# Planning, first projections and linear attention of a graph layer: three stages or one

## What is computed

```python
xn = layernorm(x)
# tconv, twice, relu between: q, k, v, s = x @ Wq + bq, ...; e = edge_attr @ We
#   logits = (q[dst] * (k[src] + e)) per head / 8; softmax over the edges of dst
#   agg = sum over edges of (v[src] + e) * a;  result = agg + s
gnn = tconv(relu(tconv(xn, ...1)), ...2)
# linear attention, 4 heads of 32
k = softmax over all nodes of (xn @ Wk_mix);  context = k^T v, per head
mix = ((xn @ Wq_mix) * 32**-0.5 @ context) @ W_out + b_out
x = x + gnn + mix
x = x + moe(layernorm(x))          # 8 experts, 2 per node
```

## Time and profile before

| | us |
|---|---|
| median of 3 runs | 4657.78 |
| the profiled execution, whole | 4652.28 |
| its span in the trace | 4650.3 |
| plan, from its first DMA issue | 2.67 to 84.59 |
| first projections | to 340.51 |
| linear attention | to 474.91 |
| first edge stage | to 2119.34 |
| second projections | to 2362.22 |
| second edge stage and experts | to the end |

### The profile page before, as it was taken

The page is one execution under the profiler, slowest core; times in us unless marked ns, Lnnn a source line. Parts: engine busy times, 40 slices in busy tenths (PEclk is TensorE's granted clock), DMA queues, the critical chain, the costliest instruction groups (busy, mean ns, idle before and its releaser), DMA issues. The chain is left out here.

```text
span 4650.3 us, 105757 instructions
## 1 busy us (share of the span) xinstructions
PE 4196.0 (90%) x19410; PEld 3412.2 (73%) x19411; DVE 3781.8 (81%) x8580; ACT 2965.7 (64%) x10488; POOL 2773.8 (60%) x2804
## 2 busy tenths in 40 slices
PE   1987899999999999997889999999999999569994
PEld 0545788888888888873368888888888888359993
DVE  3444799999999999994569999999999999755443
ACT  0111478878888878883138887887888888535331
POOL 1000777777777777760058777777777777143465
PEclk9998999999999999998999999999999999769997
DMA  4434877777777777753477777777777777252344
GB/s 78 138 131 147 236 223 226 223 216 226 223 219 221 222 215 225 225 172 111 142 214 229 220 224 214 223 225 215 221 224 223 219 226 220 93 173 78 108 139 122
DMA packets 590944, 887.02 MB, mean 191 GB/s; under 512 B 111925, under 2 KB 455797, under 8 KB 590166
## 3 DMA queue, kind: packets, MB, share of 16 engines
q0 software_dynamic: 150656, 488.11, 35.7%
q1 hardware_dynamic: 397302, 340.56, 25.3%
q10 hardware_dynamic: 42336, 51.40, 3.0%
HBM read 788.70 MB, written 91.03 MB: 189 GB/s over the span
## 5 line engine op out<-in xcount | busy, mean ns | idle before, releaser
L871 POOL DMA_INDIRECT edge_kv<-kvD,edge_ix x1760 | 1745.1, 992 | 735.4 <-issue 455.2
L918 ACT ACTIVATE edge_w<-edge_vj,edge_ex 128x64 f32<-128x64 f32 x7040 | 1857.3, 335 | 364.8 <-PE edge_pa L959 357.3
L936 PE MATMUL edge_ps<-edge_We,edge_ea 112*128 112x256 f32 x7040 | 1837.5, 383 | 43.1 <-DMA edge_ea<-ea_t_dram 17.6
L936 PEld LDWEIGHTS edge_ps<-edge_We,edge_ea 112*128 112x128 f32 x7040 | 1324.3, 190 | 283.6 <-DVE edge_prod L1071 46.8
L959 PE MATMUL edge_pa<-edge_w,edge_oh 128*128 128x260 f32 x3520 | 1091.8, 393 | 57.2 <-DVE acc L993 32.7
L940 PE MATMUL edge_ps<-acc,edge_oht 128*128 x3520 | 1055.4, 381 | 0.3 <-ACT edge_oht L886 0.3
L993 DVE TENSOR_TENSOR acc<-acc,edge_pa 128x260 f32 x1760 | 731.9, 416 | 100.6 <-PE edge_pa L959 56.1
L959 PEld LDWEIGHTS edge_pa<-edge_w,edge_oh 128*128 128x128 f32 x3520 | 631.9, 190 | 222.2 <-issue 75.4
L940 PEld LDWEIGHTS edge_ps<-acc,edge_oht 128*128 128x128 f32 x3520 | 673.7, 192 | 95.9 <-issue 1.8
L1039 DVE TENSOR_TENSOR edge_kj<-edge_kv,edge_ps 128x512 f32<-128x512 f32 x880 | 599.1, 681 | 43.7 <-PE edge_ps L940 29.0
L1071 DVE TENSOR_TENSOR edge_prod<-edge_kj,edge_ps 128x512 f32<-128x512 f32 x880 | 598.8, 680 | 0.0
(11 more groups left out here) (256 smaller groups left out, 3639.8 us busy)
## 6 DMA issues: line engine op xcount, KB each, us to landing
edge_ea<-ea_t_dram SPq DMA_DIRECT2D x1760, 112.0 KB
edge_kb<-relD SPq DMA_DIRECT2D x178, 160.0 KB
edge_kv<-kvD,edge_ix POOLq DMA_INDIRECT x1760
kvD<-nodes_kvs ACTq DMA_DIRECT2D x98, 256.0 KB
ffn_xr<-xsD SPq DMA_DIRECT2D x112, 128.0 KB, 2.1
ysD<-ffn_yo SPq DMA_DIRECT2D x112, 128.0 KB, 2.1
edge_pen<-penD SPq DMA_DIRECT2D x352, 32.0 KB
W<-W_dram SPq DMA_DIRECT2D x16, 512.0 KB, 8.2
```

Of the source, the lines that this page charges most:

```text
L871: nc.gpsimd.indirect_dma_start(out=kv[:, j % HT, :], out_offset=None, in_=g.kvD, in_offset=bass.IndirectOffsetOnAxis(ap=ix[:, h, j % HT:j ...
L918: nc.scalar.activation(w[:, j % 4, h * CA:h * CA + C], vj[:, slot, h * C:(h + 1) * C], ACT.Copy, scale=ex[:, x, h, k:k + 1])
L936: nc.tensor.matmul(ps[:, j % 4, 0:D], ea[:, j % HT, k, :], We[:, k, :], start=(k == 0), stop=(k == 1))
```

## The change

`plan`, `nodes(..., 1)` and `mix` become one stage, `opening`; its work is written out block by block over steps t = 0 to 56, without loops. In step t block t is projected, and the other work hangs on t = 7i + j:

- x is loaded ahead of the weights. TensorE transposes block t + 1 ahead of the products of block t; slots are b % 2 over all blocks, pm has one slot, kvs a ring of 4.
- The maximum runs along: after turn m, at j = 1 of the next, VectorE reduces kt (two turns are kept, not all nodes) and takes the minimum with the last (`lowest`), ScalarE at j = 2 makes the factor exp(old - new) and exp of 896 columns (`weigh`), TensorE transposes in pairs at j = 3 to 6, VectorE copies them, and one turn later seven products make a context that VectorE adds to the running one times the factor (`gathered`).
- Plan: VectorE's part in `planned(t)` at t = 0 to 8, 12 to 15 and 25 to 27; its DMAs and their waits are on ScalarE's queue at t = 10 to 28; the transposes of the tables at t = 22, 23, 29, 30.
- M goes to DRAM (MD). The output pass and resD are gone.
- `nodes(..., 2)` becomes `between`: xT of the first projections is read again, xT @ M is put into the same PSUM columns ahead of s, and b_out is added to the bias; x is read in place of resD. Relus of a turn's last two blocks move behind the first two xT copies of that turn. The first block's inputs are loaded ahead of the weights.

The diff's core (sync, PSUM tiles and evictions that stay alike are left out):

```diff
+def opening(nc, z, g, a, src_t, dst_t, dst_first):
+            def load(b):                                 # SP
+                if b >= UB:
+                    sp.wait_ge(s_xn, b - UB + 1)
+                sp.dma_start(xin[:, b % UB, :], a["x"][b * P:(b + 1) * P, :]).then_inc(s_xl[b % UB], 16)
...
+            def weigh(m):                                # ScalarE
+                act.wait_ge(s_mx, m + 1)
+                need(act, s_et, UB * m)
+                if m > 0:
+                    nc.scalar.activation(fac[:, m:m + 1], low[:, m:m + 1], ACT.Exp, bias=low[:, m + 1:m + 2], scale=-1.0).then_inc(s_fac, 1)
+                nc.scalar.activation(eb[:, :], kt[:, m % 2, :], ACT.Exp, bias=low[:, m + 1:m + 2],
+                                     accum_out=es[:, m:m + 1]).then_inc(s_eb, 1)
...
+            def planned(t):
+                if t == 10:
+                    act.wait_ge(s_tab, 1)
...
+                if t == 12:
+                    act.wait_ge(s_tst, 32)
...
+                if t == 16:
+                    act.wait_ge(s_rel, 1)
...
+                if t == 19:
+                    act.wait_ge(s_store, 64)
...
+            deviation(0)
+            for t in range(NB + UB):
+                i, j = t // UB, t % UB
+                if t < NB:
+                    x_copy(t)
+                if 0 <= t - 1 < NB:
+                    keep_mix(t - 1)
+                if t < NB:
+                    x_store(t)
+                    if j == 3 and i + 1 < NI:
+                        deviation(i + 1)
+                if 0 <= t - 2 < NB:
+                    store(t - 2)
+                if j == 2 and 0 < i <= NI:
+                    weigh(i - 1)
+                planned(t)
...
+            transpose(0)                                 # TensorE
+            for t in range(NB + UB + 1):
+                i, j = t // UB, t % UB
+                if t + 1 < NB:
+                    transpose(t + 1)
+                if j == 0 and 0 <= i - 2 < NI:
+                    context(i - 2)
+                if t in TURNED:
+                    tables(TURNED[t])
+                if 0 < i <= NI and j >= 3:
+                    turned(i - 1, pairs(j))
+                if t < NB:
+                    mixed(t)
+                    if t == 0:
+                        pe.wait_ge(s_w, 128)
+                    projected(t)
...
+            for t in range(NB + UB + 1):                 # VectorE
+                i, j = t // UB, t % UB
+                if j == 0 and 0 <= i - 2 < NI:
+                    gathered(i - 2)
+                if t in TURNED:
+                    tables(TURNED[t])
+                if 0 < i <= NI and j >= 3:
+                    copied(i - 1, pairs(j))
+                if t < NB:
+                    evicted(t)
+                if j == 1 and 0 < i <= NI:
+                    lowest(i - 1)
+                if t < NB and i + 1 < NI:
+                    if j == 1:
+                        statistics(i + 1)
...
+                planned(t)
...
+def between(nc, z, g, a):
+                    if j >= 2:                           # ScalarE, behind the xT copy
+                        if more:
+                            relu(i + 1, j - 2)
+                    elif not isinstance(i, int) or i > 0:
+                        relu(i, UB - 2 + j)
...
+                    pe.wait_ge(s_xm[j], 16 * i + 16)     # TensorE
+                    need(pe, s_ev, b - back(j, 2, UB) + 1)
+                    for c in range(2):
+                        nc.tensor.matmul(pj[:, j % 2, 3 * D:4 * D], xm[:, j, c, :], M[:, c, :], start=(c == 0), stop=False)
+                    pe.wait_ge(s_xT, b + 1)
+                    for c in range(2):
+                        nc.tensor.matmul(pj[:, j % 2, 3 * D:4 * D], xT[:, j, c, :], W[:, c, 3 * D:4 * D], start=False, stop=(c == 1))
...
-                plan(nc, z, g, a["src_t"], a["dst_t"], a["dst_first"])
-                with Stage(nc, "mixkv") as st:
-                    g.kTm, g.vm = st.sb("kTm", [P, NP]), st.sb("vm", [P, NP])
-                    nodes(nc, z, g, 1, a)
-                    mix(nc, z, g, a)
-                for layer in (1, 2):
-                    if layer == 2:
-                        nodes(nc, z, g, 2, a)
-                    edges(nc, z, g, layer, a)
+                opening(nc, z, g, a, a["src_t"], a["dst_t"], a["dst_first"])
+                edges(nc, z, g, 1, a)
+                between(nc, z, g, a)
+                edges(nc, z, g, 2, a)
```

More of the change, by code:

```diff
@@ L341, in nodes @@
+        r0 = st.sb("r0", [P, NSP])
         pj = st.ps("pj", [P, 2, 4 * D])
         pT = st.ps("pT", [P, 2, 2 * D])
[L343 to L351 removed]
@@ new lines, in _ @@
+            for b in range(UB):
+                load(b)
+            sp.dma_start(Wm[:, :, :], a["W_qkv"].rearrange("(c p) n -> p c n", p=P)[:, :, MH:3 * MH]).then_inc(s_wx, 16)
+            for n, w in enumerate(("q", "k", "v", "s")):
+                sp.dma_start(W[:, :, n * D:(n + 1) * D], a[f"W{w}1"].rearrange("(c p) n -> p c n", p=P)).then_inc(s_w, 16)
+                sp.dma_start(bias[:, n * D:(n + 1) * D], a[f"b{w}1"].partition_broadcast(P)).then_inc(s_w, 16)
+            sp.dma_start(first[:, :], dst_first.partition_broadcast(P)).then_inc(s_in, 16)
@@ new lines, in projected, with turned @@
+            def projected(b):
+                need(pe, s_ev, b - 1)
+                for n in range(2):
+                    for c in range(2):
+                        ins = nc.tensor.matmul(pj[:, b % 2, n * 2 * D:(n + 1) * 2 * D], xT[:, b % UB, c, :],
+                                               W[:, c, n * 2 * D:(n + 1) * 2 * D], start=(c == 0), stop=(c == 1))
+                ins.then_inc(s_pj, 1)
+            def turned(m, which):
+                pe.wait_ge(s_eb, m + 1)
+                need(pe, s_ek, UB * m + which[0])
+                need(pe, s_up, m)
+                if m >= 1:
+                    pe.wait_ge(s_pv, before(m))
+                for k, u in enumerate(which):
+                    nc.tensor.transpose(px[:, 1 + k, :], eb[:, u * P:(u + 1) * P], g.ident[:, :]).then_inc(s_et, 1)
@@ new lines, in before, with context, tables @@
+            def before(m):
+                return sum(t < (m + 1) * UB + 3 for t in TURNED)
+            def context(m):
+                pe.wait_ge(s_ek, UB * (m + 1))
+                for u in range(UB):
+                    ins = nc.tensor.matmul(px[:, 0, :], ek[:, u, :], vm[:, m % 2, u, :], start=(u == 0), stop=(u == UB - 1))
+                ins.then_inc(s_cx, 1)
+            def tables(n):
+                kind, lo, hi = GROUPS[n]
+                pe.wait_ge(s_rel, 1)
+                need(pe, s_pv, n)
+                pe.wait_ge(s_ek, UB * (LATE // UB - 1) if n < 2 else UB * (LATE // UB))
+                pe.wait_ge(s_up, LATE // UB - 1 if n < 2 else LATE // UB)
+                for u in range(lo, hi):
+                    ins = nc.tensor.transpose(px[:, u - lo, :], (srcF, rel)[kind][:, u, :], g.ident[:, :])
+                ins.then_inc(s_pt, 1)
@@ new lines, in _ @@
+            statistics(0)
+            dve.wait_ge(s_hd, 2)
+            linked(nc.vector.tensor_scalar(hrow[:, :], hrow[:, :], 5, None, ALU.arith_shift_right))
+            linked(nc.vector.tensor_scalar(hcol[:, :], hcol[:, :], 5, None, ALU.arith_shift_right))
+            linked(nc.vector.tensor_copy(rowf[:, :], hrow[:, 0:1]))
+            linked(nc.vector.tensor_copy(colf[:, :], hcol[:, :]))
+            inverse(0)
+            for j in range(UB):
+                normed(0, j)
+            linked(nc.vector.memset(low[:, 0:1], FAR))
@@ L1843, in build @@
     g.baseD = dram("baseD", (NP, D))
-    g.resD = dram("resD", (NP, D))
+    g.MD = dram("MD", (D, D))
     g.skipD = dram("skipD", (NP, D))
```

815 lines of the change are left out of this document (385 added, 430 removed).

## The result

The kernel after takes 4495.48 us (median of four runs, 4494.67 to 4503.66), the kernel before beside it 4655.94 (four runs, 4653.33 to 4660.43): ratio 0.9658, 95% interval 0.9642 to 0.9675. Forecast were 4501, range 4468 to 4540.

What follows compares the result with a forecast made beforehand. TensorE was taken to set the pace in the projections. Opening 301.7 us against 472.2 (-170.5) and second projections 256.6 against 242.9 (+13.7) gave -156.8: 4495.5 profiled, 4501 as median, range 4468 to 4540.

Steps and rivals of the forecast that it cites:

- Exp waits, 6 x 1.3: Opening, third block of six turns: TensorE waits 1.3 us for ScalarE's copies behind maximum, table load and exp; 7.8 us.
- VectorE's wait for the gathers: Opening, step 12: POOL's gathers may come late, but VectorE late by under a block adds no cost of its own.
- ScalarE's queue, 11.3, and 4.0 for the clock: Opening: plan waits on ScalarE's queue expose 11.3 us; slow records at lower clock after two long waits add 4.0.
- Step 18's own 0.7: Opening: the plan's three DMA issues in step 17 on ScalarE's queue expose 0.7 us.
- the keys' wait: Opening, step 19: ScalarE's wait for the keys, 13.2 us against 9.7 plus slack, exposes 4.1.
- Start, blocks, tail: Opening: start 15.0 us, first block 4.9, 48 blocks at 4.87 233.8, table transposes 1.5, serial tail 23.4.
- The second projections: Stage after the opening: 4.49 us a block, 1.6 a border, start 19.8; 256.6 against 242.9, 13.7 more.
- the waits hide: Rival: table writes and maximum come in time and clock falls are spared; 23 us less, 4478; chance 0.14.
- ScalarE's queue holds TensorE more: Rival: small-piece writes share rings with block traffic, four waits grow by 6 us each; 4525; chance 0.20.
- Not recovered: Rival: second projections don't recover their waits, 49 x 0.86 us on top of 243; 4529; chance 0.12.
- The drain: Rival: each exp table load also waits out a 1.38 us drain, seven times on the path; 4511; chance 0.05.
- The clock: Slower rival: TensorE at 1.2 instead of 2.4 GHz through both changed stages; 4960 us; chance 0.02.

Runs made afterwards that it cites:

- e4: Kernel after with an unused square root behind ScalarE's wait for the maximum, forcing exp's table load behind that wait; opening stage 297.56 us against 297.70.
- e1: Kernel after with VectorE's wait for the gathered tables moved from step 12 to step 13; opening stage 290.49 us against 297.70.
- e12: Kernel after, unchanged, run again beside the fastest version; 4496.02 us, ratio 0.9656 to the kernel before.
- e11: Kernel after with plan in later steps, slots alternating over all second-projection blocks, first copy ahead of four relus, 4-byte table writes behind last block; 4463.46 us, ratio 0.9586.
- e9: Kernel after with plan in later steps, slots alternating over all second-projection blocks, first copy ahead of four relus; 4726.24 us, ratio 0.9639 to the kernel before.
- e10: Kernel after with the tables' 4-byte-piece writes moved from step 10 behind the last block, their read to the last step; opening stage 294.55 us against 297.70.
- e6: Kernel after with two relus of the second projections put ahead of a turn's first copy again; second projections 264.23 us against 258.00.

## Why the prediction was right, and where it wasn't

- **Faster, and by what**: right. TensorE sets the pace at 4.88 a block (4.87), and the removed borders, the second pass and the output pass are gone. The opening gave -174.5 (-170.5), the second projections +15.1 (+13.7), and the stages that the change leaves alone +3.0 (0).
- **Exp waits, 6 x 1.3**: the step that failed. "Then a table load" was put behind the wait for the maximum. It lies ahead of it, and ScalarE then meets TensorE's need. With the load behind the wait (e4) the price is 1.3 to 1.4, a square root of 0.29 in it. The working was loose too: its terms up to the minimum add to 2.64 and not 2.85, and on to the copies' end to 6.2 and not 6.55, so the wait would have been 0.9 by them.
- **VectorE's wait for the gathers**: missed. The prediction let the gathers come late and put no time to them; "a VectorE late by less than a block delays TensorE only through the waits costed above" failed twice: the wait is 8.60 us, nearly two blocks, and behind it on VectorE stands the copy of the last exponential, for which the next block's context product waits. This is the second step that failed, a term put at nothing: 8.1 us, of which e1 takes 5.5 away.
- **ScalarE's queue, 11.3, and 4.0 for the clock**: steps 13, 17 and 20 cost 1.6, 6.1 and 1.4, where 2.2, 5.6 with its exp wait, and 4.1 stood; the clock 1.9 at step 18, and 1.5 in the records at 14. Step 18's own 0.7 did not show. The kind was right, the keys' wait too large.
- **Start, blocks, tail**: the start 1.0 less and the first block 1.8 more, though in e12 it is 1.1 less, so this term is open by some 3 us; 48 blocks with the tables 232.3 (277.3 - 23.5 - 21.5) where 235.3 stood, because the first turn has no transposes of exponentials; the tail 0.4 less (its terms add to 23.3, not 23.4). By the prediction's own numbers the start scales to 14.7, not 15.0.
- **The second projections** went by the prediction's steps: 4.53 (4.49) a block, 1.62 (1.6) a border, start 18.6 (19.8).
- **The rivals**: "the waits hide" came about for exp alone. In e11, with the plan later and the pieces last, another 16 us go, but 8.1 of them are the wait that it does not name. "ScalarE's queue holds TensorE more" did not come about: its steps cost 11.0 us with the clock behind them, 12.5 with the slow records of step 14, less than the 15.3 of the sum. "Not recovered" would have been 285 us in the second projections. The drain is not in the rows (e4). The clock stayed at 0.95.

Against the profiled execution the sum was 4495.5, and that execution of the kernel after took 4495.67; the 5.5 us between them and the 4501 forecast were added for the median, which now lies at the profiled time. That the sum is so near is luck in part: 7.8 us of exp waits that do not occur stand for 8.1 of a wait that was missed, an opening 4.0 shorter than forecast meets second projections 1.4 longer and unchanged stages 3.0 longer, and the opening alone differs by 4.5 us between two profiles of the same kernel (297.70 and 293.22, e12). The total alone would have proved both wrong steps right.

## What to carry to other kernels

When a side job is spread over a main loop by hand, put each wait on an in-order queue where its result is long since there, and ask of every engine that waits (VectorE here, not only the one that issues) what of the main loop is queued behind. Put writes in very small pieces where little other traffic needs the queue: here a tail of 23 us was free. And when a sum comes out right, check its terms one by one against the trace.

## What the runs showed of the hardware

- The compiled program has the table load ahead of the semaphore wait of the activation that needs it (101.69 against 106.28), so a load costs the path nothing where the engine waits for data anyway. It took 1.28 us, and 1.29 from its start to the next activation (219.73 to 221.02).
- Two writes of 896 pieces of 4 bytes, 7 KB in all, took 12.1 us to land (11.3 in e11's tail, with little beside them). In e9, in their wake, the queue moved 0.32 MB in 6 us with all 16 engines held, and right behind that VectorE stood for 4.3 and 2.5 us and ScalarE for 7.6 although, as I read the code, all that they wait for was done. The Trainium skill, page "DMA: Bandwidth & Descriptors", section "Queues, rings and completion order", says that all that one such engine issues runs on one row of rings and that each DMA engine consumes a ring's descriptors in order; so what is issued later in the row stands behind. The 100% of q10 agrees with it for the stores. That an engine stops without a wait of its own is not told by it. The one packet of the instruction queue comes at 72 to 73 us in e9 and at 68 to 69 in e10 and e11; late instruction fetch is what I suspect, but no run tested it, and that packet lies ahead of the gaps. With the pieces moved, the gaps are gone (e10 and e11, one profile each), so the pieces bring them about; by which way stays open.
- From one set of runs to the next the first edge stage, unchanged code, took 1645 us (after), 1690 (e6) or 1767 (e1), 7% more, while the second projections agree within 1.4 us. The granted clock is 0.99, 0.98 and 0.97 there, too little for it, and GB/s are 217, 211 and 202; the cause was not tried.
